# Mixture experts in groups of four, with the last four of a batch carried into the next iteration

## What is computed

```python
h = conv1d(x, cos(phases) * w_real - sin(phases) * w_imag)    # 16 taps, VALID: 735 tokens x 64
xn = layernorm(h)
q, k = xn @ Wq.T, xn @ Wk.T
h = h + softmax(q @ k.T / 8) @ xn                             # 735 x 735 per batch
xn = layernorm(h)
logits = xn @ gate_w + gate_b                                 # 16 experts
topk_w = softmax(top 2 of logits)
expert_out[e] = relu(xn @ w1[e] + b1[e]) @ w2[e] + b2[e]      # 64 -> 128 -> 64
y = xn + sum over the two chosen experts of topk_w * expert_out
out = h + layernorm(y) * gamma + beta
```

## Time and profile before

| | |
|---|---|
| median of three | 431.23 us |
| profiled execution | 430.75 us, of which its span is 428.8 us |
| TensorE busy | 397.3 us (93%) |
| VectorE busy | 252.4 us (59%) |
| ScalarE, GpSimd busy | 157.8 us (37%), 129.6 us (30%) |
| granted TensorE clock, mean | 0.988 |
| costliest group | `hidden<-up,b_neg,gates_all` on VectorE, 194 of 594 ns |

### The profile page before, as it was taken

One profiled execution on the slowest core, in us unless ns is written; L12 is line 12 of the kernel. 1 busy time (PEld: TensorE's weight loads), 2 busy tenths in 40 slices (PEclk: granted clock), 3 DMA queues, 4 the chain that ended last, 5 costly groups with the idle time before them and its releaser, 6 DMA issues.

```text
span 428.8 us, 6480 instructions
## 1 busy us (share of the span) xinstructions
PE 397.3 (93%) x2326; PEld 255.4 (60%) x2326; DVE 252.4 (59%) x607; ACT 157.8 (37%) x486; POOL 129.6 (30%) x158
## 2 busy tenths in 40 slices
PE   8889887999999999999999999999999889988892
PEld 6676554766576656666575657665666556555450
DVE  3273556458745775458545874478555964464772
ACT  1346412433263325433354335341553333232121
POOL 3100300104323442146125432244215620553601
PEclk9999969999999999999999999999999999999998
DMA  6500004910096004900194007700292019401940
GB/s 184 136 0 2 1 2 150 415 39 0 8 337 262 18 2 189 409 26 2 58 393 170 5 4 289 311 20 0 73 412 104 0 39 375 174 3 41 373 174 18
DMA packets 22847, 55.93 MB, mean 130 GB/s; under 512 B 3744, under 2 KB 4768, under 8 KB 22688
## 3 DMA queue, kind: packets, MB, share of 16 engines
q1 hardware_dynamic: 22816, 55.53, 34.4%
HBM read 53.57 MB, written 1.95 MB: 129 GB/s over the span
## 4 chain that ended last, share of the span: by engine, by line
PE 68%; DVE 22%; ACT 4%; issue 3%; DMA 1%; POOL 1%; POOLq 0%; SPq 0%; DVEq 0%; ACTq 0%
PE mix L880 18%; PE up L880 17%; PE wide L880 14%; PE small L880 13%; DVE row_max L720 5%; DVE hidden L782 4%; PE wide L906 3%; DVE x L659 2%; ACT x L469 1%; PE wide L1030 1%; DVE top_at L753 1%; DVE q_lo L659 1%; DVE xn L672 1%; PE wide L982 1%; PE small L899 1%
## 5 line engine op out<-in xcount | busy, mean ns | idle before, releaser
L782 DVE SCALAR_TENSOR_TENSOR hidden<-up,b_neg,gates_all 128x368 f32<-128x368 f32 x194 | 107.3, 594 | 92.8 <-PE up L880 83.6
L880 PE MATMUL mix<-hidden,w2s 128*64 128x368 f32 x512 | 94.1, 485 | 1.7 <-DVE hidden L782 1.7
L880 PE MATMUL up<-x,w_hi 128*128 128x368 f32 x236 | 87.9, 372 | 1.4 <-DVE hidden L782 0.9
L880 PE MATMUL up<-x,w_lo 128*128 128x368 f32 x236 | 77.8, 329 | 0.0
L416 POOL TENSOR_SCALAR var_eps<-var 128x6 f32<-128x6 f32 x24 | 5.8, 242 | 204.7 <-ACT cen_sq L494 204.7
L880 PEld LDWEIGHTS up<-x,w_hi 128*128 128x128 f32 x236 | 44.3, 188 | 25.0 <-issue 13.1
L880 PEld LDWEIGHTS mix<-hidden,w2s 128*64 128x64 f32 x512 | 31.0, 136 | 39.3 <-issue 27.9
L539 ACT ACTIVATE probs<-wide 128x736 f32<-128x736 f32 (+2 forms) x48 | 36.7, 785 | 42.5 <-PE wide L880 42.5
L302 POOL TENSOR_TENSOR hidden<-relu,gates_all 128x368 f32<-128x368 f32 x42 | 40.5, 984 | 39.1 <-ACT relu L531 24.8
L720 DVE TENSOR_REDUCE row_max<-wide 128x1 f32<-128x736 f32 (+1 forms) x48 | 42.2, 912 | 10.7 <-PE wide L880 10.6
L880 PEld LDWEIGHTS up<-x,w_lo 128*128 128x128 f32 x236 | 44.6, 189 | 0.0
(11 more groups left out here) (136 smaller groups left out, 468.2 us busy)
## 6 DMA issues: line engine op xcount, KB each, us to landing
gates_all<-gates_far SPq DMA_DIRECT2D x128, 368.0 KB, 8.3
xt<-x_t SPq DMA_DIRECT2D x8, 375.0 KB, 12.1
out<-outs SPq DMA_DIRECT2D x8, 192.0 KB, 1.8
w_raw<-w SPq DMA_DIRECT2D x2, 512.0 KB, 6.5
w2s<-w SPq DMA_DIRECT2D x1, 512.0 KB, 7.4
gates_far<-gates_t SPq DMA_DIRECT2D x8, 46.0 KB, 1.7
gates_all<-w_real SPq DMA_DIRECT2D x1, 256.0 KB, 2.8
gates_all<-w_imag SPq DMA_DIRECT2D x1, 256.0 KB, 2.9
```

Source lines behind the costliest of these rows:

```text
L782: dve.scalar_tensor_tensor(hidden[:, e % HIDDEN, s, :], up_of(e, tail)[s], b1_neg[:, e:e + 1], gates_all[:, e, s * HALF:(s + 1) * HALF], A ...
L880: return pe.matmul(dst, lhsT, rhs, start=start, stop=stop, skip_group_check=True)
```

## The change

- Experts are handled in four groups of four. First layers of a group stand beside other fp32r work, and its four second layers follow in one block with the values or the convolution.
- Experts 12 to 15 of batch m (`SPLIT` = 12) are no longer in iteration i but in iteration i + 1, beside scores 0 to 3 of batch i + 1; there m's predecessor is called `before`. Gate transposes, `gates_to_rows`, the broadcast, the mix copy, the transposes of the convolved batch and `h0_copy` go to iteration i + 1 with them.
- `keys` and `keys1` have two buffers, and `keys_hi` no longer waits for the exponentials. The transposed maxima stand in `wide[0]`, scores use the order `SCORE_BUF`.
- `POOLED` is (4, 8, 9, 10) for (10, 13, 14). In iterations with attention ScalarE and GpSimd do these experts; in the last mixture VectorE does GpSimd's part, as before.
- The last mixture computes its experts in threes (after the four that are left over), the convolution is cut in two parts (3 and 5 of 8 chunks).

The removed bodies of the iterations are those printed above; `...` stands for lines left out.

```diff
-POOLED = (10, 13, 14)
+POOLED = (4, 8, 9, 10)
 HIDDEN = 4
-CONV_CUTS = (0, 3, 5, CHUNKS)
-MAX_BUF = (1, 0, 1, 0, 0, 1)
-MAX_FREE = (0, 0, 1, 2, 4, 3)
+QUAD = 4
+SPLIT = E - QUAD
+CONV_FIRST = 3
+MAX_BUF = (1, 0, 1, 0, 0, 0)
+MAX_FREE = (0, 0, 1, 2, 4, 5)
+SCORE_BUF = (1, 0, 1, 0, 0, 1)
+SCORE_FREE = (0, 0, 1, 2, 4, 3)
...
-        keys = sb("keys", [P, TOKP], F32R)
+        keys = [sb(f"keys_{k}", [P, TOKP], F32R) for k in range(2)]
...
# SP
             def iteration(i, par, first, att, conv, ahead):
+                if not first:
+                    broadcast(i - 1, 1 - par, True)
                 if ahead:
                     load_next(i + 2, par)
                 if not first:
                     store(i - 2)
-                if att:
-                    broadcast(i, par, True)
...
# GpSimd
+                if conv:
+                    deviation(0, i + 1)
                 if not first:
                     pool.wait_ge(s_ftc, CREDIT + i - 1)
                     pool.tensor_tensor(cen2[:], moe_tok[:], xn2[par][:, :, 0:D], ALU.add).then_inc(s_cen[2], 1)
-                if conv:
-                    deviation(0, i + 1)
-                if not first:
                     deviation(2, i - 2)
                     gamma_beta(i - 2, par)
...
+                gate_hidden(pool, i - 1, POOLED[0])
                 deviation(1, i)
-                gate_hidden(pool, i - 1, POOLED[0])
...
# ScalarE, new iteration
+                m, before = i - 1, i - 2
+                if not first:
+                    gates_to_rows(m, True)
                 if att:
                     shift(i)
+                if conv and not first:
+                    act.wait_ge(s_h1, i)
+                    h0_copy(i + 1, 1 - par)
                 if att:
                     exponentials(i, 0, 2)
                 if conv:
                     variance(0, cen0[1 - par], i + 1)
                 if att:
+                    exponentials(i, 2, 4)
+                if not first:
+                    mix_copy(before)
                 if conv:
                     keys_hi(i + 1)
                     keys_hi_again(i + 1)
                 if att:
+                    exponentials(i, 4, NT)
+                if not first:
+                    act.wait_ge(s_ft, CREDIT + before + 1)
+                    act.wait_ge(s_cen[2], CREDIT + before)
+                    tokens_copy(moe_tok, s_ftc)
+                if conv:
+                    query_hi(i + 1)
+                if not att:
+                    rectify(m, POOLED[0], True)
+                if not first:
+                    variance(2, cen2, before)
+                if att:
                     attention_copy(i)
+                    rectify(m, POOLED[0], False)
                     variance(1, cen1, i)
                     x2_hi(i, par)
+                for e in POOLED[1:]:
+                    rectify(m, e, not att)
                 if att:
                     exp_gap(i)
                 if ahead:
                     conv_copy(i + 2)
...
# VectorE, new iteration (att; in the last one: experts 12 to 15 of batch 6, then 0 to 15 of batch 7)
+                if not first:
+                    hide_both(before, SPLIT, True)
                 if conv:
                     centre(i + 1, 1 - par)
+                if not first:
+                    for e in range(SPLIT + 1, E):
+                        hide_both(before, e, True)
                 if conv:
                     normalise(0, xn1[1 - par], cen0[1 - par], i + 1)
+                hide_both(m, 0, True)
                 if conv:
                     keys_lo(i + 1)
+                for e in range(1, 4):
+                    hide_both(m, e, True)
                 if conv:
                     query_lo(i + 1)
+                scale_attention(i)
+                centre_sum(i, par)
+                hide_both(m, 4, True)
+                # then, with conv, reduce_max 0; hide 5; reduce_max 1; hide 6; reduce_max 2; hide 7; reduce_max 3
...
+                dve.wait_ge(s_cen[2], CREDIT + i - 1)
+                normalise(1, xn2[par], cen1, i)
+                x2_lo(i, par)
+                for e in range(8, 11):
+                    hide_both(m, e, True)
+                if conv:
+                    reduce_max(i + 1, 4, MAX_BUF[4])
+                top_two(i)
+                top_places(i)
+                gate(i)
+                hide_both(m, 11, True)
+                if conv:
+                    reduce_max(i + 1, 5, MAX_BUF[5])
...
# TensorE
             def scores(i, t):
...
-                    pe.wait_ge(s_prob, NT * i + t - 1)
+                    pe.wait_ge(s_prob, NT * i + SCORE_FREE[t])
...
             def last_mixture(n, buf):
+                transpose_gates(n)
+                first_layer(n - 1, 12, 1 - buf, True)
+                first_layer(n - 1, 13, 1 - buf, True)
+                pe.wait_ge(s_gtc, BATCH)
+                first_layer(n - 1, 14, 1 - buf, True)
+                first_layer(n - 1, 15, 1 - buf, True)
                 first_layer(n, 0, buf, True)
+                first_layer(n, 1, buf, True)
+                for e in range(SPLIT, E):
+                    second_layer(n - 1, e)
+                for e in range(2, 5):
+                    first_layer(n, e, buf, True)
                 pe.wait_ge(s_mixc, CREDIT + n)
                 pe.wait_ge(s_attn, BATCH)
                 to_tokens(moe_t, s_ft)
                 gated_biases(n)
                 second_layer(n, 0)
+                second_layer(n, 1)
+                for e in range(5, 14, 3):
+                    for k in range(e, e + 3):
+                        first_layer(n, k, buf, True)
+                    for k in range(e - 3, e):
+                        second_layer(n, k)
+                first_layer(n, 14, buf, True)
+                first_layer(n, 15, buf, True)
+                for e in range(11, E):
+                    second_layer(n, e)
...
             def iteration(i, par, first, att, conv, ahead):
+                if not first:
+                    transpose_gates(m)
+                transpose_max(i)
+                if not first:
+                    first_layer(before, 12, par)
+                    if conv:
+                        pe.wait_ge(s_convc, i + 2)
+                        to_tokens(conv_t, s_ht)
                 pe.wait_ge(s_gtc, i)
+                scores(i, 0)
+                if not first:
+                    first_layer(before, 13, par)
+                scores(i, 1)
+                if not first:
+                    first_layer(before, 14, par)
+                scores(i, 2)
+                if not first:
+                    first_layer(before, 15, par)
+                scores(i, 3)
+                if not first:
+                    for e in range(SPLIT, E):
+                        second_layer(before, e)
+                first_layer(m, 0, buf)
+                if conv:
+                    pe.wait_ge(s_ln[0], i + 2)
+                    pe.wait_ge(s_prob, NT * i + 3)
+                    to_features(wide[1], xn1[1 - par], s_t1)
+                scores(i, 4)
+                first_layer(m, 1, buf)
+                if conv:
+                    pe.wait_ge(s_khi, i + 2)
+                    pe.wait_ge(s_kone, i + 2)
+                    pe.wait_ge(s_klo, i + 2)
+                scores(i, 5)
+                first_layer(m, 2, buf)
...
+                    to_tokens(moe_t, s_ft)
+                first_layer(m, 3, buf)
+                if conv:
+                    pe.wait_ge(s_prob, NT * i + 5)
+                    project(i + 1)
+                pe.wait_ge(s_ftc, CREDIT + m)
+                for t in range(NT):
+                    weigh_values(i, t, par)
+                gated_biases(m)
+                for e in range(4):
+                    second_layer(m, e)
+                attention_to_tokens(i)
+                first_layer(m, 4, buf)
+                if conv:
+                    next_max(i, 0)
+                    next_max(i, 1)
+                first_layer(m, 5, buf)
+                if conv:
+                    next_max(i, 2)
+                first_layer(m, 6, buf)
+                if conv:
+                    next_max(i, 3)
+                first_layer(m, 7, buf)
+                if ahead:
+                    pe.wait_ge(s_attn, i + 1)
+                    convolve(i + 2, par, 0, CONV_FIRST)
+                for e in range(4, 8):
+                    second_layer(m, e)
                 pe.wait_ge(s_ln[1], i + 1)
                 if conv:
                     pe.wait_ge(s_max, NT * i + NT + 3)
                 to_features(wide[1], xn2[par], s_t2)
+                first_layer(m, 8, buf)
+                if conv:
+                    next_max(i, 4)
+                first_layer(m, 9, buf)
                 gate_logits(i, par)
+                first_layer(m, 10, buf)
+                if conv:
+                    next_max(i, 5)
+                first_layer(m, 11, buf)
+                if ahead:
```

(3 more changed lines are left out.)

203 lines of the change are left out of this document (52 added, 151 removed).

## The result

The changed kernel takes **438.94 us** (median of four, 437.4 to 439.08) against 430.99 (429.41 to 431.54) for the kernel before on the same chip: ratio 1.018, interval 1.015 to 1.022. It is slower, with the whole interval above 1. The direction was forecast; 438.94 lies 2.5 us above the range (428.4 to 436.4) and 6.3 above the forecast of 432.6. The profiled execution took 439.02 with a span of 437.2 (before: 430.75 and 428.8).

A forecast was written before the change was run, and what follows sets the result against it. Bound: TensorE's issue, changes of kind and late VectorE releases. Content 42.9 plus waits gave 47.3 per steady iteration; with both ends, +1.4 on the profiled 430.75 made 432.2, or 432.6 on the median; range 428.4 to 436.4.

The forecast's parts named there:

- Iteration 1, 44.4 us: Iteration 1, without leftover experts: ends at 117.1 for 119.42; four experts less worth 5.2, new stall 2.9.
- the clock's fall: Rival, 25%: TensorE's clock falls in iteration 1, 6.8 us of work at half speed, about +3.2, so 435.8.
- the stretch that it named, 73.3 to 81.2: Part of iteration 1 where the clock rival expected the fall, with about 4.3 of 7.9 us of work in flight.
- The steady iteration, 47.3 us: Iterations 2 to 5: content 42.9 plus listed waits, 0.42 more than 46.86 each, +1.7 over four.
- four fewer turns, 0.34 each: Steady iterations: fp32 blocks go from eight to four, a round trip costs 0.34; 1.5 us saved per iteration.
- The largest stall: Experts 4 to 7 beside maxima 0 to 3: TensorE alternates with VectorE's hides and maxima, 1.68 us lost.
- Iteration 6: No convolution there: 44.3 us, with last-block waits of 0.7 for GpSimd's expert 10 and 0.8 for hide 11.
- Iteration 7: No keys, queries or maxima there: 40.2 us, experts 4 to 7 ending at 27.3, hide 11 awaited until 39.5.
- The opening: Start of the kernel: two records fewer in the bias product, -0.2; maxima's transposes at 72.7 for 72.92.
- The last mixture: End of the kernel, now 20 experts: 30.6 us, mix copy 30.8 after iteration 7, at 421.6 for 420.15.
- the rival that they come later: Rival, 8%: gates arrive later than 11.1, or the last mixture waits over 1.9 for them; 431 to 435.
- Late expert gating: Rival, 12%: GpSimd's three successive experts, 5.7 us, exceed their cover; 1 us lost in each of five iterations, 437.6.

The follow-up runs named there:

- e10: Changed kernel with second layer 12 ahead of first layer 15, one turn more per iteration 2 to 6; 438.27 us (1.019).
- e5: Changed kernel with empty matmuls in iteration 1 alone, 3 ahead of the first scores and 11 ahead of the next batch's transposes; 436.62 us (1.015).
- e2: Changed kernel with ScalarE's variance of the next batch ahead of exponentials 0 and 1 in iteration 1 alone; 435.38 us (1.012).
- e3: Changed kernel with VectorE's hidden of expert 13 ahead of its two centre operations; 439.48 us (1.023).
- e9: Changed kernel with 4 empty matmuls behind each of the opening's last five key-block maxima, none in iteration 1; 439.21 us (1.019).
- e6: Changed kernel with the four 16-row products of the gates' biases ahead of the attention values; 437.40 us (1.015).
- e14: Changed kernel with the moves of e2, e6, e8 and e13, first layer 8 before the second LayerNorm's transposes, gate logits behind first layer 10; 426.41 us (0.989).
- e8: Changed kernel with the convolution's chunks 0 to 2 between first layers 5 and 6, in iterations 1 to 5; 436.33 us (1.014).
- e13: Changed kernel with second layers 14 and 15 between first layer 1 and scores 5, mixture copy behind exponential 4; 435.54 us (1.010).

## Why the prediction was wrong

- **Iteration 1, 44.4 us: the step that failed.** The step put the clock's fall at nothing and kept it as a rival (25%, 435.8). Without the fall the same order takes 45.07, so the bookkeeping of the waits was short by 0.7 (the longest of them was right: the transposes of the next batch come 8.5 after its start in e10, forecast 8.6); the fall adds 3.6 in the profiled execution. By these figures 438.94 would have been some 435.3 without it, inside the range. e5 and e2 show it from both sides: fill the waits or remove them, and most of the loss goes.
 The rival was nearer, but not right in its terms. It priced 6.8 us of lower clock at 3.2; the table gives 1.7 for that (e3), and the stretch was 17.07 long. That 3.2 came close to 3.6 is luck, two errors that offset each other. Nor did the fall come from the stretch that it named, 73.3 to 81.2: it began at 71.22, behind the opening's last maxima, whose order the kernel before shares. In 12 of the 14 profiled executions with the changed kernel's opening a fall began between 69.4 and 72.7, in the two of the old order none did; why is not shown. The named stretch, with its wait of 2.67, can only have kept the clock down; in e3 (78.30) and e9 (84.05) a fall does begin there.
 The Trainium skill (TensorE: Matmul & The Clock Gate, "HAM oscillation — how this bites in real kernels") says that a burst behind a long enough wait starts at the lower clock. The traces of e3 and e9 agree, where the matmuls behind that wait run at 0.50; in e10 the same wait is followed by 1.00. No run here tells what decides between 0 and 17 us in the same order.
- **The steady iteration, 47.3 us: a term mis-sized.** The mechanism was right: four fewer turns, 0.34 each (e10: 0.34), eaten by waits. The largest stall was at experts 4 to 7, as worked out (6.63 for 6.48). Missing were the 16-row matmuls' own change of kind inside the value block, part of the 0.31 by which the stretch from the values to the spread matmul was longer (e6 gets 0.15 back), and 0.14 and 0.15 at the first scores and at experts 4 to 7; behind these 0.17 was regained, which leaves 0.44. Four times 0.44 is 1.8. How the rest of the 0.31 arises stays open.
- **Iteration 6** was 0.4 late by its spread matmul already, for the same reasons. The waits at its end, for GpSimd's expert 10 and hide 11, were 0.57 and 1.02 for 0.7 and 0.8; the other 0.4 I did not trace. **Iteration 7** was 0.6 late by the spread matmul and 0.9 by the end of first layer 7 (28.2 for 27.3), where first layers wait for relu 4 and for hides 5 and 6 (0.32, 0.23 and 0.18); its last 0.3 is not traced.
- **The opening**, forecast -0.2, was -1.33. That is no gain of the change: the low stretch at 57 lasted 3.41 us for 6.83. In e9, with 6.83, the gates' transposes came at 64.52, in the kernel before at 64.54, in the changed kernel at 63.22.
- **The last mixture**, 30.8, was 30.76. (The prediction's terms add up to 30.7 and are given as 30.6, and 30.8 went into the sum.) Its first new hidden came 7.02 after its gate transposes for 7.4; VectorE's rows, the changed kernel and e14:

```profile
404.81 1.11 DVE L789 SCALAR_TENSOR_TENSOR hidden<-wide,b_neg,gates_all 128x368 f32<-128x368 f32 x2 [1.67 <-PE mix L900]
```

```profile
392.54 1.11 DVE L794 SCALAR_TENSOR_TENSOR hidden<-wide,b_neg,gates_all 128x368 f32<-128x368 f32 x2 [1.41 <-DMA gates_all<-gates_far]
```

 The first row names TensorE, but the second layer that frees this buffer is the first of four from 402.70 on, and so done a microsecond before. The gates' loads are issued from 401.21 on, and the quickest takes 3.5 us to land, which is 404.7; in e14 the same wait is put down to them. So the gates released it, 0.4 sooner than forecast, and the rival that they come later did not come true.
- **Late expert gating** was a rival at 12%, and did not come true. GpSimd's three gatings and, beside them, VectorE's gap and the gates it leads to:

```profile
254.13 5.63 POOL L301 TENSOR_TENSOR hidden<-relu,gates_all 128x368 f32<-128x368 f32 x6 [6.59 <-ACT relu L528]
```

```profile
257.01 0.93 DVE L756 TENSOR_TENSOR gap<-top 128x6 f32<-128x6 f32 x1
...
260.34 0.25 DVE L781 TENSOR_TENSOR gates<-pick,wide 128x96 f32<-128x96 f32 x1
```

 A six-element operation (per partition) took 0.93, where the six-element ones around it take 0.16 to 0.20. In the kernel before, where GpSimd is idle at that point, it took 0.17:

```profile
251.07 0.17 DVE L749 TENSOR_TENSOR gap<-top 128x6 f32<-128x6 f32 x1
```

 The gates were still ready 2.9 before their transposes at 263.49, so nothing waited. The Trainium skill (SBUF — State Buffer, "SBUF: two separate sides") says of a VectorE operation with two SBUF inputs and a GpSimd operation that reads SBUF that one excludes the other for a whole instruction. The 0.93 beside gatings of 0.94 each agrees, and it stayed off the path.
- **Where the expected gain went.** In the kernel before, second layers and other work stood between first layers and covered the round trip through the one pair of `up` buffers. Putting second layers in fours saves turns and uncovers that round trip. e8 puts work back into it, e13 into the wait for the keys, and e14 has both, e6's order and two further moves, and keeps most of the fours: 47.74 goes to 45.82, while two of the turns saved are paid again.
- **In total**, after less before by the spans of the profiled executions, 437.2 - 428.8 = +8.4: the clock in iteration 1 +3.6; iterations 2 to 7 +3.3; opening, iteration 1 without the fall, and a last mixture with four experts more -1.3 - 1.4 + 4.3 = +1.5 (rounded terms). Without the fall the kernel would still be slower, by some 4.8.
- **The chances.** Slower had 0.62 and was right. The range was too narrow since it added the clock's fall to no other miss: the fall and the steady iterations together, 432.6 + 3.6 + 1.8 = 438.0, lie outside it.

## What to carry to other kernels

Before grouping work of one kind, list what each of its pieces covered: a saved turn of 0.34 us is lost if it bares a buffer's round trip of 0.6. Where an edit thins out a stretch after an opening, treat a fall of TensorE's clock as part of the forecast, not as a rival, and reorder the producers of the wait before filling it. Judge moves of a few tenths by the distance between two boundaries in the profile, since runs of one kernel can lie more than 1% apart (e3: 438.16 us at a granted clock of 0.990, 443.36 at 0.967).

## What was not expected of the hardware

- The same instruction order had 0, 6.83, 10.24 and 17.07 us of lower clock in iteration 1 in different executions, and took 45.07 to 48.67 us.
- Steady iterations repeat within 0.03 us (47.73 to 47.76).
- Four 16-row matmuls among 64-column ones cost a change of their own: 0.76 us for 0.62, and 0.15 of the iteration came back when e6 moved them.
